# A graph-attention and expert kernel on one core: gathers without the other block's rows, one word of block numbers for two groups, and the message's wait last

## The chip, the cores and the metric

The kernel runs on one core of one Trainium2 chip. The core has five engines: PE (TensorE, matmuls), DVE (VectorE), ACT (ScalarE), POOL (GpSimd) and SP (SyncE, which only issues DMAs here), and 16 DMA engines. Each engine has a sequencer of its own that also carries out register operations, waits and branches. The metric is the device time of one execution in microseconds, the median of several runs: 3036.38 us before the change.

## The reference, cut to what matters

```python
def _gat_layer(x, W, attn_l, attn_r, bias, src, dst, num_heads, head_dim, use_elu):
    z = (x @ W).reshape(N, num_heads, head_dim)
    el = jnp.sum(z * attn_l, axis=-1); er = jnp.sum(z * attn_r, axis=-1)
    e = jax.nn.leaky_relu(el[src] + er[dst], 0.2)
    ex = jnp.exp(e - segment_max(e, dst)[dst])
    alpha = ex / segment_sum(ex, dst)[dst]
    out = segment_sum(alpha[:, :, None] * z[src], dst) + z + bias
    ...                                   # elu in the first two layers
x = x + gat(gat(gat(layernorm(x))))       # 3125 nodes, 768 wide, 50000 edges; heads 12, 12, 1
x = x + experts(layernorm(x))             # 8 experts, the best 2 of each token, 768 -> 192 -> 768
```

The edges are sorted by dst. Everything is float32.

## The kernel before

Each of the three graph layers is a *node sweep* and an *edge sweep*. The node sweep multiplies the 25 blocks of 128 nodes by W and stores z with its el (and a second, scaled el) as a row of a table in HBM. The edge sweep sums the messages. The rest (router, experts) comes after the third layer and isn't touched.

**Tiles and visits.** The 50000 sorted edges are 391 tiles of 128 edges. A tile whose edges end in two different blocks of destination nodes is *visited* twice, once for each block: 391 + 24 = 415 visits, `V`. Five visits are a group (`G`), 83 groups (`NG`) a layer; four groups are one turn of a hardware loop and have 20 buffers of rows (`U`). Block numbers of the visits aren't known when the program is built: they lie in `b_of` and are loaded into registers.

**One visit k**, in the order in which its data flow:
- POOL (line 672) gathers the 128 table rows of the tile's source nodes by an indirect DMA into buffer k mod 20, as soon as PE has added up visit k - 20 (semaphore `s_agg`). At a tile's second visit the same 128 rows are fetched again.
- PE (line 1022) fetches er of the edges' destinations by three small matmuls for each visit, with the transposed one-hot tile ST_b; it does so three groups ahead (`ER_LEAD`), for visits 0 and 1 behind visit 1 and for visits 2 to 4 behind visit 3, and then signals `s_er`.
- DVE (lines 1475 and 1480 in the layers with 12 heads, 1457 to 1469 in the last) makes the logits of a whole group; it waits for `s_er` and for the five gathers (`s_z`). ACT exponentiates (lines 821, 822).
- DVE (line 1492) multiplies each row by its weights, 768 numbers: the message, `s_msg`. In the last layer the weight goes into the one-hot tile instead (1494, 1498).
- For five or six visits of 20 (`SPLIT`) ACT and DVE split the row into a leading and a remaining part (781, 1509), so that PE adds it by four fast matmuls rather than by two slow ones; the semaphore is `s_rest`. These are called split visits here. SPLIT is places 2, 7, 10, 12, 17 of 20 in the first two layers and 1, 4, 7, 11, 14, 17 in the last.
- PE (line 1047) adds the row, turned by the one-hot tile S, onto the block's sums in PSUM, two halves of 384 or so. An edge of the other block has no 1 in its row of S, so its message is multiplied by zero.
- ACT (`close`) moves a finished block's sums out.

PE's program for a group is written out by `body`: load the block numbers of group g (`now`), visit 0, load those of group g + 3 (`later`), visit 1, six er matmuls, visits 2 and 3, nine er matmuls, visit 4. Ahead of each visit's matmuls stand its waits: the message or the rest, then `s_acc_free` (the block's sums are free, line 1042), and for visit 0 `s_S` (line 1044).

The tables by visit (`src_k`, `dst_k`, `b_of`) are made once, by DVE, ahead of the first node sweep; PE waits for them (`s_tables`).

Of the kernel before, what the change touches and what calls it, by code (L numbers as in the profile page):

```python
# [8 lines left out]
I32 = mybir.dt.int32  # L9
U32 = mybir.dt.uint32  # L10
U8 = mybir.dt.uint8
ALU = mybir.AluOpType
# [3 lines left out]
P = 128  # L16
N, D = 3125, 768
NE = 50000
NB = -(-N // P)
NPAD = NB * P  # L20
# [5 lines left out]
G = 5  # L26
NBUF = 4
IN_ARENA = 3
ER_LEAD = 3
U = G * NBUF  # L30
VISITS = ET + NB - 1
V = -(-VISITS // G) * G
NG = V // G
# [23 lines left out]
class Chain:  # L57
# [5 lines left out]
    def link(self, instruction):  # L63

        self.mark(instruction)
        self.follow()
# [33 lines left out]
def gnn_ffn(nc, x, edges, gnn, ffn, out):  # L100
    with ExitStack() as ctx:
        def sb(name, shape, dt=F32):
            return ctx.enter_context(nc.sbuf_tensor(name, shape, dt))
# [62 lines left out]
        src_k = sb("src_k", [P, V], I32)  # L166
        dst_k = sb("dst_k", [P, V])
        b_k = sb("b_k", [1, V + 1], I32)
        b_g = sb("b_g", [1, NG, 4], I32)
        b_of = sb("b_of", [1, NG + ER_LEAD, 8], I32)  # L170
        ends = sb("ends", [1, NB], I32)
        turns = sb("turns", [1, NS], I32)
# [171 lines left out]
        def prep(at, n):  # L344
            return ST[:, :, :, :].rearrange("p a b c -> p (a b c)")[:, at:at + n]
# [4 lines left out]
        def bk_f():  # L350
            return prep(V, V)
# [230 lines left out]
        def _(pool):  # L582
# [70 lines left out]
            for l in range(3):  # L653
                if l == 1:
                    pool.wait_ge(s_base, 16 * NB)
                    pool.wait_ge(s_spare, 16)
                    pool.wait_ge(s_last_bias, 16)
                if l == 2:
                    pool.wait_ge(s_bias_added, 16 * NB)
                sweep_nodes(pool, [(store(l), 0)])  # L660
                pool.wait_ge(s_stored[0], 16 * (NB // 2 + 1) * (l + 1))
                pool.wait_ge(s_stored[1], 16 * (NB // 2) * (l + 1))
                pool.wait_ge(s_tab, NB * (l + 1))
                pool.wait_ge(s_tables, 1)
                pool.wait_ge(s_filled, 16 * 2 * 3)
                pool.sem_inc(s_tick)
                for k in range(V):
                    pool.wait_ge(s_agg, V * l + k + 1)
                    if l == 2 and k == 12 * D // slot_width(l):
                        for q in range(2):  # L670
                            pool.wait_ge(s_x_kept[q], 16 * (NB // 2 + 1 - q))
                    nc.gpsimd.indirect_dma_start(  # L672
                        edge_row(l, k % U)[:, 0:table_width(l)], None, table[l][:, :],
                        bass.IndirectOffsetOnAxis(src_k[:, k:k + 1].bitcast(U32), 0)).then_inc(s_z[k % U], 16)

            for b in range(NB):
                keep_rows(b)
# [251 lines left out]
        def _(pe):  # L929
# [74 lines left out]
            def edge_sweep(l):  # L1004
# [5 lines left out]
                def blocks_of(g):  # L1010

                    return nc.values_load_multi_w_load_instructions(
                        b_of[0:1, bass.ds(g, 1), 0:G].rearrange("o i j -> o (i j)"), engines=[mybir.EngineType.PE],
                        min_val=0, max_val=NB - 1,
                        skip_runtime_bounds_check_because="b(k) is a sum of NB - 1 comparisons")[1]

                def er_of_edges(g, jj, j, b):

# [9 lines left out]
                def add_up(g, i, jj, j, b):  # L1028

                    at = jj * G + j  # L1030
                    odd = (b + l) % 2
                    flat = PS[:, :, :].rearrange("p b n -> p (b n)")
                    if at in SPLIT[l]:
                        n = SPLIT[l].index(at)
                        pe.wait_ge(s_rest, len(SPLIT[l]) * i + (n + 1 + split_before(l)))
                        onehot = S[:, jj, j, :]
                        rows = [parts[:, n, part, :] for part in range(2)]
                    else:
                        pe.wait_ge(s_msg, g * G + (V * l + j + 1))
                        onehot = f32(S[:, jj, j, :]) if H > 1 else S_weighted[:, jj, j, :]  # L1040
                        rows = [edge_row(l, at)]
                    pe.wait_ge(s_acc_free, b + (NB * l + 1))
                    if H > 1 and j == 0:
                        pe.wait_ge(s_S, g + (NG * l + 1))
                    for c, n in ((0, HALF), (1, sum_width(l) - HALF)):
                        for row in rows:
                            o = nc.tensor.matmul(flat[:, bass.ds(odd * 1024 + 512 * c, n)], onehot,  # L1047
                                                 row[:, c * HALF:c * HALF + n], start=False, stop=True, skip_group_check=True)
                    o.then_inc(s_agg, 1)

                def body(i, last):
                    groups = LAST_GROUPS if last else NBUF
                    for jj in range(groups):
                        g = NBUF * i + jj
                        ahead = not last or jj + ER_LEAD < groups
                        now = blocks_of(g)
                        for j in range(G):
                            add_up(g, i, jj, j, now[j])
                            if j == 0 and ahead:
                                later = blocks_of(g + ER_LEAD)  # L1060
                            if j in (1, 3) and ahead:
                                for n in ((0, 1), (2, 3, 4))[j // 2]:
                                    er_of_edges(g + ER_LEAD, (jj + ER_LEAD) % NBUF, n, later[n])

                pe.wait_ge(s_erm, l + 1)
                for g in range(ER_LEAD):
                    now = blocks_of(g)
                    for j in range(G):
                        er_of_edges(g, g, j, now[j])
# [129 lines left out]
        def _(dve):  # L1199
# [61 lines left out]
            link(nc.vector.tensor_copy(b_of[0:1, 0:NG, 0:G], starts))  # L1261
# [16 lines left out]

            def tables():
                dve.wait_ge(s_turned, 1)  # L1280
                link(nc.vector.tensor_copy(src_k[:, :], PS[:, 2, 0:V]))
                link(nc.vector.scalar_tensor_tensor(out=dst_k[:, :], in0=bk_f(), scalar=-float(P), in1=PS[:, 3, 0:V],
                                                    op0=ALU.mult, op1=ALU.add))
                if V > VISITS:
                    link(nc.vector.memset(dst_k[:, VISITS:V], NO_NODE))
                dve.sem_inc(s_tables, 1)

            W_parts = [(l, k, j) for l in (1, 2) for k in range(KC) for j in range(2)]
# [150 lines left out]
            def edge_sweep(l):  # L1439
# [8 lines left out]
                def exponents(g, i, jj):  # L1448
# [28 lines left out]

                    def higher():
                        dc.follow()
                        nc.vector.tensor_tensor(t, u, wu[:, :, H:2 * H], ALU.max).then_inc(s_pre, 1)  # L1480

                    if H > 1:
                        return both_logits, higher
# [376 lines left out]
```

## Time and profile before

| | us |
|---|---|
| median of 3 runs | 3036.38 |
| lowest, highest | 3032.83, 3039.52 |
| span of the profiled execution (no other time of it is given) | 3059.8 |
| PE busy in it | 2691.3 (88%) |
| DVE, POOL, ACT busy | 2096.8 (69%), 1506.0 (49%), 1244.9 (41%) |
| mean granted clock of PE, as a share | 0.964 |
| HBM read and written | 640.01 MB and 133.45 MB |

The span lies 0.8% over the median. It is counted from the first instruction to the last of one execution taken by the hardware profiler. Ends of matmuls are modelled, since they are pipelined, so a busy PE need not be one at its peak; the same matmul appears as several records. "Issue" is time in which an engine waited for nothing that the profile shows: its sequencer was at something else. "Remote" or "unknown queue" is a release whose event isn't among the recorded ones.

### The profile page before, as it was taken

Reading aid. Unit: us, or ns where it says so; the run is one execution under the profiler, and the core shown is the slowest. Engines: PE = TensorE matmul, PEld = TensorE weight load, DVE = VectorE, ACT = ScalarE, POOL = GpSimd, SP = SyncE. Lnnn points to the kernel's source line nnn. Section 1 sums busy time; section 2 is a strip of 40 time slices with the busy share of each in tenths; the row PEclk is TensorE's granted clock in tenths of the full one; section 3 lists DMA queues with packets and bytes.
Section 4 is the critical chain, followed back from the end, with each engine's and each line's share of the span. In section 5 each row is a group of like instructions: output and inputs, shape, how many; then the busy total and the mean of one; then the engine's idle time right before and its main releaser. Section 6 shows DMA issues by size and latency. Waiting matters only on the chain.

```text
span 3059.8 us, 57119 instructions
## 1 busy us (share of the span) xinstructions
PE 2691.3 (88%) x14056; PEld 1838.6 (60%) x14060; DVE 2096.8 (69%) x3895; ACT 1244.9 (41%) x2607; POOL 1506.0 (49%) x1528
## 2 busy tenths in 40 slices
PE   3997999998989979898989999788898889759998
PEld 2884555555558855555555578555555555547776
DVE  6776888888887768888878877545555555673332
ACT  1224555555544435555555544223222223622211
POOL 1005666666631156666666412466666665114443
PEclk9998999999999979999999999899999999979999
DMA  6447888888867878888888767788888887967776
GB/s 210 169 148 251 289 286 291 291 290 290 289 219 205 210 228 292 289 287 290 291 287 288 250 191 216 218 281 285 279 282 281 282 282 258 397 217 145 145 146 118
DMA packets 199261, 762.09 MB, mean 249 GB/s; under 512 B 41889, under 2 KB 58033, under 8 KB 198542
## 3 DMA queue, kind: packets, MB, share of 16 engines
q0 software_dynamic: 127632, 604.14, 64.8%
q1 hardware_dynamic: 53790, 108.21, 11.6%
q10 hardware_dynamic: 17760, 48.79, 4.0%
q8 instruction: 36, 0.59, 0.1%
q14 instruction: 43, 0.35, 0.0%
HBM read 640.01 MB, written 133.45 MB: 253 GB/s over the span
## 4 chain that ended last, share of the span: by engine, by line
PE 50%; DVE 21%; issue 13%; ACT 4%; DMA 4%; another core or an unknown queue 3%; SPq 2%; POOL 1%; DVEq 1%; ACTq 1%; POOLq 0%
PE PS L1047 30%; DVE arena L1492 5%; PE PS L1176 5%; PE PS L978 4%; PE PS L1165 4%; PE PS L980 2%; DVE parts L1509 2%; PE PS L1022 2%; DMA arena<-table,src_k 2%; SPq L493 1%; DVE ST_b L1445 1%; DVE arena L1357 1%; DVE arena L1367 1%; DVE arena L1335 1%
## 5 line engine op out<-in xcount | busy, mean ns | idle before, releaser
L672 POOL DMA_INDIRECT arena<-table,src_k x945 | 959.9, 1016 | 500.8 <-issue 213.1
L1047 PE MATMUL PS<-arena,S 128*128 128x384 f32 (+1 forms) x1848 | 706.8, 514 | 57.8 <-issue 46.3
L1492 DVE TENSOR_TENSOR arena<-arena,PS 128x768 f32<-128x768 f32 x630 | 575.2, 946 | 0.9 <-ACT arena L822 0.9
L1047 PEld LDWEIGHTS PS<-arena,S 128*128 128x128 f32 x1848 | 335.5, 194 | 282.7 <-issue 156.8
L1047 PE MATMUL PS<-parts,S 128*128 128x384 f32 (+2 forms) x1332 | 340.4, 375 | 57.2 <-issue 51.0
L672 POOL DMA_INDIRECT W<-table,src_k x300 | 295.9, 986 | 160.5 <-PE PS L1047 71.2
L1047 PE MATMUL PS<-arena,S_weighted 128*128 128x384 f32 (+1 forms) x840 | 319.9, 516 | 33.4 <-issue 25.3
L1022 PEld LDWEIGHTS PS<-erp,ST_b 128*128 128x128 bf16 x3735 | 193.9, 97 | 249.9 <-issue 184.2
L618 POOL DMA_DIRECT2D table<-arena x75 | 41.6, 555 | 557.7 <-DVEq L1379 382.3
L1047 PEld LDWEIGHTS PS<-parts,S 128*128 128x128 f32 x1332 | 223.7, 192 | 106.0 <-issue 97.5
L830 ACT ACTIVATE apart<-iota_row,dst_k 128x128 f32<-128x128 f32 x830 | 261.7, 389 | 60.8 <-issue 44.1
L781 ACT ACTIVATE parts<-arena 128x780 fp32r<-128x780 f32 x168 | 142.0, 849 | 309.2 <-DVE arena L1492 136.7
L1022 PE MATMUL PS<-erp,ST_b 128*128 x3735 | 213.0, 172 | 54.0 <-issue 38.9
L1047 PE MATMUL PS<-W,S 128*128 128x396 f32 (+1 forms) x640 | 239.8, 502 | 14.6 <-issue 8.1
L1047 PEld LDWEIGHTS PS<-arena,S_weighted 128*128 128x128 f32 x840 | 154.3, 196 | 143.7 <-issue 79.4
L978 PE MATMUL PS<-W_lead,S 128*128 128x512 f32 x450 | 190.4, 423 | 9.8 <-DVE xT_rest L1383 7.9
L1509 DVE TENSOR_TENSOR parts<-arena,parts 128x780 fp32r<-128x780 f32 x168 | 162.0, 964 | 35.7 <-issue 24.4
L1492 DVE TENSOR_TENSOR W<-W,PS 128x768 f32<-128x768 f32 x200 | 182.4, 944 | 0.0
L978 PE MATMUL PS<-W_lead,xT_rest 128*128 128x512 f32 x450 | 179.2, 398 | 0.0
L978 PE MATMUL PS<-W_rest_r,S 128*128 128x512 f32 x450 | 178.7, 397 | 0.0
L1047 PEld LDWEIGHTS PS<-W,S 128*128 128x128 f32 x640 | 116.1, 190 | 91.3 <-issue 39.0
L1795 DVE TENSOR_SCALAR arena<-PS,gate_of 128x768 f32<-128x768 f32 x56 | 57.0, 1018 | 162.5 <-PE PS L1176 162.5
(293 smaller groups left out, 4354.1 us busy)
## 6 DMA issues: line engine op xcount, KB each, us to landing
arena<-mixed SPq DMA_DIRECT2D x63, 384.0 KB, 3.6
table<-arena POOLq DMA_DIRECT2D x50, 396.0 KB, 3.3
local_b<-local SPq DMA_DIRECT2D x123, 160.0 KB
mixed<-sums ACTq DMA_DIRECT2D x50, 384.0 KB
arena<-table SPq DMA_DIRECT2D x50, 384.0 KB, 4.6
arena<-table,src_k POOLq DMA_INDIRECT x945
table<-arena POOLq DMA_DIRECT2D x25, 384.5 KB, 4.6
out<-last_bias POOLq DMA_DIRECT2D x25, 384.0 KB, 6.4
```

The costliest lines, as they stand in the source:

```text
L672: nc.gpsimd.indirect_dma_start(edge_row(l, k % U)[:, 0:table_width(l)], None, table[l][:, :], bass.IndirectOffsetOnAxis(src_k[:, k:k + 1]. ...
L781: nc.scalar.activation(parts[:, n, 0, 0:D + H], row[:, 0:D + H], ACT.Copy).then_inc(s_leading, 1)
L830: o = nc.scalar.activation(apart[:, j, :], iota_row[:, :], ACT.Abs, scale=-1.0, bias=dst_k[:, bass.ds(g * G + j, 1)])
L978: nc.tensor.matmul(PS[:, 4 + 2 * b.q, :], rows[x_part], W_parts[W_part][:, 0:512], start=start, stop=stop)
L980: o = nc.tensor.matmul(PS[:, 5 + 2 * b.q, 0:z_width(l) - 512], rows[x_part], W_parts[W_part][:, 512:z_width(l)], start=start, stop=stop)
L1022: o = nc.tensor.matmul(er_of(l, jj)[:, j, :], ST_b[:, jj, j * P:(j + 1) * P], erp[:, bass.ds(b * (6 * H) + part * 2 * H, 2 * H)], start=(p ...
L1047: o = nc.tensor.matmul(flat[:, bass.ds(odd * 1024 + 512 * c, n)], onehot, row[:, c * HALF:c * HALF + n], start=False, stop=True, skip_grou ...
L1165: o = nc.tensor.matmul(to, token_xT(b.q)[:, k * P:(k + 1) * P], WiT[:, k, bass.ds(e * FF, FF)], start=(k == 0), stop=(k == KC - 1))
L1176: o = nc.tensor.matmul(PS[:, 4 + 2 * b.q + c, 0:HALF], hT(b.q)[0:rows, j * P:(j + 1) * P], flat[0:rows, bass.ds(e * (2 * D) + (2 * c + j) ...
L1492: nc.vector.tensor_tensor(z, z, a, ALU.mult).then_inc(s_msg, 1)
L1509: nc.vector.tensor_tensor(low[:, 0:D + H], row[:, 0:D + H], f32(high[:, 0:D + H]), ALU.subtract).then_inc(s_rest, 1)
L1795: nc.vector.tensor_scalar(zr(b.q, D).rearrange("p (c d) -> p c d", c=2), PS[:, 4 + 2 * b.q:6 + 2 * b.q, 0:HALF], gate_of[:, bass.ds(b.n, 1 ...
```

## The change

1. `src_k`: from visit 20 on, an edge that isn't of the visit's block gets 3200 added to its source number, and the gather gets a bound (`bounds_check`), beyond which a row isn't fetched. What was in the buffer stays there; the one-hot tile multiplies it by zero as before.
2. `b_of` holds for each visit the block number and, times 256, that of the visit three groups on. PE loads five words at the head of a group and takes the one by a mask and the other by a shift; the load behind visit 0 goes.
3. In `add_up` the waits for `s_acc_free` and `s_S` stand ahead of those for the message or the rest.
4. The higher of the two logits is also limited to 0, in the same instruction, so that what is left in a buffer can't overflow. b_g and turns become bytes.

```diff
-        b_of = sb("b_of", [1, NG + ER_LEAD, 8], I32)
+        b_of = sb("b_of", [1, NG, 8], I32)
...
-                        bass.IndirectOffsetOnAxis(src_k[:, k:k + 1].bitcast(U32), 0)).then_inc(s_z[k % U], 16)
+                        bass.IndirectOffsetOnAxis(src_k[:, k:k + 1].bitcast(U32), 0),
+                        bounds_check=NPAD - 1, oob_is_err=False).then_inc(s_z[k % U], 16)
...
+                def now(word):
+                    return (word & (LOW - 1)).with_bounds(min_val=0, max_val=NB - 1)
+
+                def later(word):
+                    return (word >> 8).with_bounds(min_val=0, max_val=NB - 1)
...
+                    pe.wait_ge(s_acc_free, b + (NB * l + 1))
+                    if H > 1 and j == 0:
+                        pe.wait_ge(s_S, g + (NG * l + 1))
                     if at in SPLIT[l]:
...
-                    pe.wait_ge(s_acc_free, b + (NB * l + 1))
-                    if H > 1 and j == 0:
-                        pe.wait_ge(s_S, g + (NG * l + 1))
...
-                        now = blocks_of(g)
+                        words = blocks_of(g)
                         for j in range(G):
-                            add_up(g, i, jj, j, now[j])
-                            if j == 0 and ahead:
-                                later = blocks_of(g + ER_LEAD)
+                            add_up(g, i, jj, j, now(words[j]))
                             if j in (1, 3) and ahead:
                                 for n in ((0, 1), (2, 3, 4))[j // 2]:
-                                    er_of_edges(g + ER_LEAD, (jj + ER_LEAD) % NBUF, n, later[n])
+                                    er_of_edges(g + ER_LEAD, (jj + ER_LEAD) % NBUF, n, later(words[n]))
...
+            link(nc.vector.scalar_tensor_tensor(out=b_of[0:1, 0:NG - ER_LEAD, 0:G], in0=blocks[:, ER_LEAD:, :], scalar=float(LOW),
+                                                in1=blocks[:, 0:NG - ER_LEAD, :], op0=ALU.mult, op1=ALU.add))
...
-                link(nc.vector.tensor_copy(src_k[:, :], PS[:, 2, 0:V]))
...
+                link(nc.vector.tensor_copy(src_k[:, 0:U], PS[:, 2, 0:U]))
+                below, beyond = prep(2 * V, V - U), prep(3 * V, V - U)
+                link(nc.vector.tensor_scalar(below, dst_k[:, U:], 0.0, float(NPAD), ALU.is_lt, ALU.mult))
+                link(nc.vector.tensor_scalar(beyond, dst_k[:, U:], float(P), float(NPAD), ALU.is_ge, ALU.mult))
+                link(nc.vector.tensor_tensor(below, below, beyond, ALU.add))
+                link(nc.vector.tensor_tensor(src_k[:, U:], below, PS[:, 2, U:V], ALU.add))
...
-                        nc.vector.tensor_tensor(t, u, wu[:, :, H:2 * H], ALU.max).then_inc(s_pre, 1)
+                        nc.vector.scalar_tensor_tensor(out=t, in0=u, scalar=0.0, in1=wu[:, :, H:2 * H],
+                                                       op0=ALU.min, op1=ALU.max).then_inc(s_pre, 1)
```

PE's program at the head of the loop over groups, layer 0, visits 0 and 1 of its first group, before (ISA and REGISTER_ALU are register operations; a wait stands with the instruction that carries it):

```order
L1012 TENSOR_LOAD b_of
L1039 ISA
L1042 REGISTER_ALU [waits s_msg]
L1044 REGISTER_ALU [waits s_acc_free]
L1047 ISA [waits s_S]
L1047 MATMUL PS<-arena,S 128x384
L1047 ISA
L1047 MATMUL PS<-arena,S 128x396
L1012 ISA
L1012 TENSOR_LOAD b_of
L1039 REGISTER_ALU
L1042 REGISTER_ALU [waits s_msg]
```

The same place now:

```order
L1014 TENSOR_LOAD b_of
L1041 REGISTER_ALU x2
L1043 REGISTER_ALU [waits s_acc_free]
L1050 ISA [waits s_S]
L1055 ISA [waits s_msg]
L1055 MATMUL PS<-arena,S 128x384
L1055 ISA
L1055 MATMUL PS<-arena,S 128x396
L1041 REGISTER_ALU x2
L1050 REGISTER_ALU [waits s_acc_free]
L1055 ISA [waits s_msg]
```

The second load and the operation ahead of it are gone, the mask is the first of the two REGISTER_ALU of line 1041, and the message's wait has moved behind the others, to the operation just ahead of the matmul.

DVE's making of the tables, ahead of the first node sweep, before:

```order
L1342 TENSOR_TENSOR W_rest_r<-W,W_lead 128x792 [waits s_W_lead] x5
L1281 CAST src_k<-PS 128x415 [waits s_turned]
L1282 SCALAR_TENSOR_TENSOR dst_k<-ST,PS 128x415 [waits s_dve]
L1402 MEMSET gm 128x12 [waits s_dve]
L1310 BN_STATS stats<-arena 128x6 [waits s_in0,s_dve]
```

And now:

```order
L1290 SCALAR_TENSOR_TENSOR dst_k<-ST,PS 128x415 [waits s_turned]
L1294 CAST src_k<-PS 128x20 [waits s_dve]
L1296 TENSOR_SCALAR ST<-dst_k 128x395 [waits s_dve]
L1297 TENSOR_SCALAR ST<-dst_k 128x395 [waits s_dve]
L1298 TENSOR_TENSOR ST<-ST 128x395 [waits s_dve]
L1299 TENSOR_TENSOR src_k<-ST,PS 128x395 [waits s_dve]
```

One pass over the source numbers became five instructions, four of them over 395 columns, each waiting for the one before.

## Rows read from the trace of the kernel before

**Rows 1.** Windows: stretch, length, busy us by engine (instructions), clock, DMA share, GB/s

```profile
256.00:857.00 601.00, 541.90 (x2681) 323.56 (x2682) 497.63 (x717) 326.42 (x780) 397.83 (x392) 0.97 0.88 289
1100.00:1730.00 630.00, 555.03 (x2803) 333.80 (x2804) 523.23 (x757) 339.59 (x806) 415.30 (x411) 0.97 0.88 287
1945.00:2610.00 665.00, 582.00 (x2934) 357.50 (x2933) 351.06 (x1106) 186.87 (x409) 415.07 (x418) 0.96 0.86 277
...
2601.00:2677.50 76.50, 56.04 (x377) 39.40 (x377) 51.53 (x136) 46.20 (x83) 10.91 (x20) 0.91 1.01 397
```

**Rows 2.** Chain of waits, shares by line: first, second and third edge sweep

```profile
by line: PE PS L1047 59.5%; issue 13.2%; DVE arena L1492 7.6%; another core or an unknown queue 4.1%; PE PS L1022 4.1%; DVE parts L1509 3.0%; DMA arena<-table,src_k 2.4%; DVE W L1492 1.8%; DVE ST_b L1445 1.7%; POOL arena L672 0.8%; DVE wt L
by line: PE PS L1047 28.9%; issue 18.3%; DVE arena L1492 16.3%; another core or an unknown queue 6.4%; DVE parts L1509 6.2%; DVE W L1492 4.4%; DMA arena<-table,src_k 4.0%; POOL arena L672 3.6%; DVE ST_b L1445 3.5%; PE PS L1022 1.7%; DVE wt 
by line: PE PS L1047 50.1%; issue 24.5%; another core or an unknown queue 3.7%; PE PS L1022 3.6%; DMA arena<-table,src_k 3.0%; ACT parts L785 2.1%; DVE S_weighted L1498 1.4%; DVE ST_b L1445 1.3%; ACTq L790 1.0%; DVE parts L1513 0.9%; POOL a
```

**Rows 3.** Waits of PE from 306 to 765 us: total us, times, longest

```profile
PE PS L1047 <- issue: 31.4, 75, 3.7
PE PS L1022 <- issue: 6.6, 15, 0.9
PE PS L1047 <- DVE arena L1492: 0.7, 3, 0.3
```

**Rows 4.** PE's register operations by line: ns min/median/max, first and last start

```profile
L1012 PEldq TENSOR_LOAD <-b_of x498: 5/582/1751, 249.9 to 2596.9; - x166
L1042 PEldq ALU_OP  x1245: 2/32/737, 260.9 to 2601.5; - x178
```

**Rows 5.** PE in order of time, layer 0, then layer 2: start, us, work

```profile
470.01 0.97 PE L1047 MATMUL PS<-parts,S 128*128 128x384 f32 x4
471.25 1.57 PE L1047 MATMUL PS<-arena,S 128*128 128x384 f32 x4 [0.27 <-issue]
...
472.81 0.95 PE L1047 MATMUL PS<-parts,S 128*128 128x384 f32 x4
473.60 1.47 PE L1047 MATMUL PS<-arena,S 128*128 128x384 f32 x4
...
2100.22 1.16 PE L1047 MATMUL PS<-parts,S 128*128 128x384 f32 x4
2101.23 0.45 PE L1022 MATMUL PS<-erp,ST_b 128*128 x6
```

**Rows 6.** PE's weight loads in order of time, with the idle time before

```profile
704.33 0.62 PEld L1047 LDWEIGHTS PS<-arena,S 128*128 128x128 f32 x3 [0.33 <-issue]
```

**Rows 7.** DMA queues: packets, MB, share of the 16 engines' span

```profile
q0 software_dynamic: 127632, 604.14, 64.8%
```

**Rows 8.** DVE's waits before its logits: us, times

```profile
  remote: 142.3, 85
  DMA arena<-table,src_k: 26.2, 17
```

**Rows 9.** POOL's indirect DMAs: by line, and in order of time

```profile
L672 POOL DMA_INDIRECT arena<-table,src_k x945: 941/950/1745, 246.3 to 2588.6; - x189
...
L650 POOL DMA_INDIRECT out<-arena,target_of x56 | 89.1, 1591 | 159.2 <-DMA out<-arena,target_of 124.6 <-DVE arena L1795 30.1 <-issue 4.5
L635 POOL DMA_INDIRECT arena<-normed,token_of x56 | 55.0, 983 | 53.3 <-DVE token_of L1747 30.7 <-issue 16.5 <-PE PS L1149 6.2
...
510.38 0.95 POOL L672 DMA_INDIRECT arena<-table,src_k  x1 [0.30 <-issue]
```

**Rows 10.** DVE ahead of the first node sweep, in order of time

```profile
51.16 0.58 DVE L1281 CAST src_k<-PS 128x415 int32<-128x415 f32 x1
...
54.24 0.56 DVE L1310 BATCH_NORM_STATS2 stats<-arena 128x6 f32<-128x384 f32 x1 [1.63 <-DMA arena<-in_x]
```

**Rows 11.** DVE's two forms over five columns

```profile
L1461 DVE SCALAR_TENSOR_TENSOR wu<-wu 128x5 f32<-128x5 f32 x83 | 13.5, 162 | 0.0
...
L1457 DVE TENSOR_TENSOR wu<-arena,PS 128x5 f32<-128x5 f32 x63 | 10.3, 164 | 151.6 <-remote 123.2 <-issue 17.7 <-DMA arena<-table,src_k 10.6
```

More of the change, by code:

```diff
@@ L29 @@
 ER_LEAD = 3
+LOW = 256
 U = G * NBUF
@@ L168, in gnn_ffn @@
         b_k = sb("b_k", [1, V + 1], I32)
-        b_g = sb("b_g", [1, NG, 4], I32)
-        b_of = sb("b_of", [1, NG + ER_LEAD, 8], I32)
+        b_g = sb("b_g", [1, NG, 4], U8)
+        b_of = sb("b_of", [1, NG, 8], I32)
         ends = sb("ends", [1, NB], I32)
-        turns = sb("turns", [1, NS], I32)
+        turns = sb("turns", [1, NS], U8)
         erm = sb("erm", [P, NB, 2 * HMAX])
@@ L1013, in blocks_of @@
                         b_of[0:1, bass.ds(g, 1), 0:G].rearrange("o i j -> o (i j)"), engines=[mybir.EngineType.PE],
-                        min_val=0, max_val=NB - 1,
+                        min_val=0, max_val=(NB - 1) * (LOW + 1),
                         skip_runtime_bounds_check_because="b(k) is a sum of NB - 1 comparisons")[1]
+                def now(word):
+                    return (word & (LOW - 1)).with_bounds(min_val=0, max_val=NB - 1)
+                def later(word):
+                    return (word >> 8).with_bounds(min_val=0, max_val=NB - 1)
                 def er_of_edges(g, jj, j, b):
@@ L1055, in body @@
                         ahead = not last or jj + ER_LEAD < groups
-                        now = blocks_of(g)
+                        words = blocks_of(g)
                         for j in range(G):
-                            add_up(g, i, jj, j, now[j])
-                            if j == 0 and ahead:
-                                later = blocks_of(g + ER_LEAD)
+                            add_up(g, i, jj, j, now(words[j]))
                             if j in (1, 3) and ahead:
                                 for n in ((0, 1), (2, 3, 4))[j // 2]:
-                                    er_of_edges(g + ER_LEAD, (jj + ER_LEAD) % NBUF, n, later[n])
+                                    er_of_edges(g + ER_LEAD, (jj + ER_LEAD) % NBUF, n, later(words[n]))
                 pe.wait_ge(s_erm, l + 1)
                 for g in range(ER_LEAD):
-                    now = blocks_of(g)
+                    words = blocks_of(g)
                     for j in range(G):
-                        er_of_edges(g, g, j, now[j])
+                        er_of_edges(g, g, j, now(words[j]))
                 with pe.Fori(0, NI - 1) as i:
@@ L1260, in _ @@
             link(nc.vector.memset(b_of[0:1, :, :], 0))
-            link(nc.vector.tensor_copy(b_of[0:1, 0:NG, 0:G], starts))
+            link(nc.vector.tensor_copy(b_of[0:1, :, 0:G], starts))
+            blocks = bk_f()[0:1, :].rearrange("o (g j) -> o g j", j=G)
+            link(nc.vector.scalar_tensor_tensor(out=b_of[0:1, 0:NG - ER_LEAD, 0:G], in0=blocks[:, ER_LEAD:, :], scalar=float(LOW),
+                                                in1=blocks[:, 0:NG - ER_LEAD, :], op0=ALU.mult, op1=ALU.add))
             link(nc.vector.tensor_copy(ends[0:1, 0:NB - 1], enter[0:1, :]))
```

## The prediction

> **What bounds the kernel now.** I read the page's slices and the windows by stage first, then the chain of waits stage by stage, then PE's row of instructions inside a sweep, and last POOL and DVE. The windows show five stretches [rows 1]: the three edge sweeps take 601, 630 and 665 us, 1896 of 3059.8, and the other stages hardly touch what the change touches. In a sweep three things are close to full at once: PE is busy 88 to 90%, the 16 DMA engines 86 to 88%, DVE 83% in two sweeps and 53% in the third. So busy shares don't decide it; the chain does. In the three sweeps it runs through PE's adding matmuls, the er matmuls and "issue" for 77, 49 and 78% [rows 2], 68% on average, and through landings of gathers ("DMA arena<-table" and "unknown queue") for 6.5, 10.4 and 6.7%, which is 39 + 66 + 45 = 150 us. PE first, landings second.
>
> "Issue" on PE is worth a look: PE waits for no other engine there (31.4 us before its adding matmuls in one 459 us window, 0.7 us for DVE's messages [rows 3]). The register instructions of its sequencer stand between the matmuls: a load of block numbers lasts 582 ns (498 of them), an ALU operation 32 ns, both up to 0.7 us and more at times [rows 4].
>
> **The load that goes.** Before, each group of five visits has two loads, one ahead of visit 0 and one behind it; after, one, ahead of visit 0. 498 loads become 3 x (3 + 83) = 258, so 240 go, 240 x 0.582 = 140 us of the sequencer. Most of that is hidden, since a visit of plain matmuls gives the array 1.3 us of work. It shows where the load meets a split visit, which is short: the split visit at 472.81 is followed after 0.79 us, the one at 470.01, which has the later load behind it, after 1.24 us with 0.27 idle [rows 5]. That is 0.45 us. In layers 0 and 1 it holds for places 10 of 20, about 21 groups each; in layer 2 the split visit is the one behind the load (places 1 and 11), where the er matmuls that need the load start 2101.23 - 2100.22 = 1.01 us behind the split visit instead of 0.79, 0.22 us; about 42 groups. 42 x 0.45 + 42 x 0.22 = 28 us. Bounds: 0, if something else is late there anyway, and 140.
>
> The Trainium skill (page "Runtime: NRT & Kernel Launch", section Instruction fetch mechanics) puts a register load at about 200 ns for each register, even in bulk; for five words that would be 1.0 us a load and 240 us for the 240. The row has 0.58 us for five words, so the measurement decides and I leave the page's figure out of the sum.
>
> **The register operations that come.** Each visit gets one more (the mask), in the order's listing five a group; the shift for the er matmuls takes a place that was there. Lower bound: 0, hidden under the array. Upper: idle of the weight loads before a visit, 0.33 us where nothing else is late [rows 6], holds three such operations, so about 0.1 us each; it can only show behind the nine er matmuls, once a group, 249 x 0.1 = 25 us. I take the instruction's own 32 ns: 8 us.
>
> **Pauses.** Operations of 32 ns that last 0.7 us [rows 4] are stalls of the sequencer that no engine explains. A sequencer with 0.58 - 5 x 0.1 = 0.1 to 0.58 - 5 x 0.03 = 0.4 us a group to spare recovers from some. PE's idle before lines 1047 and 1022 is 31.4 + 6.6 us in that window [rows 3], 38 of 459, so about 157 in 1896. I give 13 of them back. Bounds 0 and 80.
>
> These three, -28 + 8 - 13 = -33, count where PE is on the chain, 68%: **-22 us**. Behind a faster PE the next that is late is DVE, at 497.63 of 601 us in the first sweep [rows 1].
>
> **The waits reordered.** s_acc_free and s_S now stand ahead of s_msg. They are met long before in nearly every visit; behind the message's wait there are then one operation less or two, 0.1 us, and PE waits for a message 3 times in the window, 0.7 us [rows 3]. Queued behind the wait are this visit's matmuls and the next er matmuls, as before. -1 us, bounds 0 and -10.
>
> **Gathers with rows left out.** There are 415 visits for 391 tiles, so 24 tiles are visited twice; the first 20 visits stay whole, which leaves 23 pairs. A pair now fetches each row once: 23 x 128 + 48 rows of padding = 2992 rows a layer of 53120, 5.6%; at 3168 and 3076 bytes 28.2 MB of the queue's 604.14. That queue's packets took 64.8% of the engines' span, 1983 us, or 3.28 us for a MB [rows 7], so 93 us of transfers go. What of it lies on the chain? Landings are 150 us of it; 5.6% of that is **-8 us**. DVE's waits before its logits are booked mostly to "remote", 142.3 us, and only 26.2 us to a gather [rows 8], so a late gather isn't proven as their cause; the s_er semaphore is in the same wait. Bounds 0 and -93.
>
> By the Trainium skill ("DMA: Bandwidth & Descriptors", section Anatomy of one DMA) a DMA from POOL costs about 2.0 us fixed and bytes / 436 GB/s. The fixed part stays for a gather of half the rows; the 28.2 MB would be worth at most 65 us, not 93. The case with full gain below would shrink by that much.
>
> POOL's instruction itself: 950 ns at the median, and 0.30 us of issue between two [rows 9]. PE's pace is 1896 / 1245 = 1.52 us a visit, so POOL has 0.27 us to spare a visit. That a check of 128 indices costs POOL something is not in the trace. Bounds: 0 (the same instruction with one more field; below nothing too, if fewer rows mean fewer descriptors, with no effect, as POOL waits anyway), and the scatter's 1591 ns. I take 0, since the other indirect read, of another width, stands at 983 ns.
>
> **Ahead of the first sweep.** b_of gets one more pass over 400 numbers (0.58 us, as the row of 415 columns in [rows 10]); the table of sources becomes five instructions instead of one: 0.58 goes, four of nearly 0.58 and a short one come, some +2.0 us [rows 10]. PE waits for s_tables, but DVE's next work, on the first rows of x, starts at 54.24 after a wait of 1.63 us for them, which takes up most of it. So +1.0 us; bounds 0 and 2.6. DVE's min-and-max in place of max: a two-operation form of 5 columns has 162 ns against 164 [rows 11], so 0.
>
> **Sum.** -22 - 1 - 8 + 1 = -30 us against the profiled 3059.8, which becomes 3030. The profiled execution lies 23 us over the median of 3036.4; that part is the same in both, so 3036.4 - 30 = **3006 us**, 1.0% less.
>
> **Rivals.** (A) The forecast, 50%, with a range of its own from 2980 to 3029.
> (B) Landings and DMA traffic bound the sweeps: 88% busy engines and the "remote" waits speak for it, a stretch with 1.01 and 397 GB/s elsewhere [rows 1] against it. Then the 93 us come in full, and half of A's PE part: 3036 - 93 - 11 = 2932. 12%.
> (C) Nothing to measure: the sequencer's saved loads are spent on 1245 more operations, each 0.1 us (125 us against 140), and the rows left out shorten gathers that were in time: -5 to +5, 3036. 20%.
> (D) Slower, on POOL: with the bounds check the gather's instruction passes 1.22 us; from there POOL is the pace of a sweep. At the scatter's 1.59 + 0.30 = 1.89 us the sweeps take 1245 x 1.89 = 2353 us, +457; at 1.35 + 0.30, 1245 x 0.13 = +162. Against it: the program has the same number of POOL instructions, and an index compare is small. 7%, at about 3200.
> (E) Slower, on PE's sequencer: the operations land where they show, behind the nine er matmuls (+25), and the load's 0.45 us was not on the chain (0): 3036 + 25 - 9 = 3052. 11%.
> That rows are not left out at all (no index beyond the bound) is a case of C in time; the trace would show it in bytes.
>
> **How the numbers follow.** Measurement of this kernel tells 0.2%, 6 us, from nothing. Faster: A, B and a little of C, 66%. Same: most of C, 16%. Slower: D, E, 18%. The range for 8 in 10 reaches down towards B and up over C and E: 2935 to 3050.
>
> **What would show it.** Right: 258 loads of b_of; the split visit with the later load followed after 0.8 us, not 1.24; PE's "issue" in the sweeps down by some tens of us; software queue at about 576 MB; L673's instruction still at 950 ns with longer waits for PE. Wrong: a gather instruction over 1.2 us (D); bytes unchanged; the visit behind nine er matmuls 0.1 us later than before and PE's issue no smaller (C, E); sweeps shorter by 30 us each with DVE's "remote" wait gone (B). If PE's rows improve and the sweeps don't shorten, what I took for PE's chain was a loop through DVE and POOL.

## The result: 2.0% slower, and the profile after

The changed kernel takes 3097.5 us against 3037.1 of the kernel before, ratio 1.0201 (95% interval 1.0185 to 1.0216). The forecast was 3006, so it was wrong in sign: 60 us lost instead of 30 gained.

The windows of the three edge sweeps after (stretch, length, busy us by engine, clock, DMA share, GB/s), against [rows 1]:

```profile
256.00:868.00 612.00, 546.08 (x2707) 332.20 (x2707) 494.09 (x723) 328.57 (x781) 431.14 (x394) 0.95 0.84 272
1112.00:1750.00 638.00, 559.30 (x2776) 338.99 (x2776) 512.49 (x748) 337.35 (x799) 440.56 (x406) 0.95 0.83 267
1970.00:2645.00 675.00, 579.54 (x2928) 359.50 (x2926) 349.62 (x1106) 185.25 (x408) 449.84 (x417) 0.94 0.81 258
```

Of the 40 us between the two profiled executions 29 lie in these: the sweeps are 11, 8 and 10 us longer, DMA is 4 to 5 points less busy, and POOL 33, 25 and 35 us busier. No other engine comes near that: PE's matmuls are 4, 4 and -2 us busier, at a clock that fell by 0.02. The page's rows of the software queue and of the gathers (count, busy us, mean ns, idle before), against [rows 7]:

```profile
q0 software_dynamic: 127632, 576.01, 62.2%
...
L673 POOL DMA_INDIRECT arena<-table,src_k x945 | 1024.1, 1084 | 453.6 <-issue 244.2
...
L673 POOL DMA_INDIRECT W<-table,src_k x300 | 330.5, 1102 | 142.5 <-issue 73.7
```

and by duration (min/median/max ns), against [rows 9]:

```profile
L673 POOL DMA_INDIRECT arena<-table,src_k x945: 992/1002/1791, 247.6 to 2623.7; - x189
```

The rows that the change leaves out are left out: 576.0 MB, as forecast. But each gather's instruction takes 1.00 us at the median instead of 0.95, and on the mean of all 1245 it takes (1024.1 + 330.5) / 1245 = 1.088 us. The same two rows of the page before read:

```profile
L672 POOL DMA_INDIRECT arena<-table,src_k x945 | 959.9, 1016 | 500.8 <-issue 213.1
...
L672 POOL DMA_INDIRECT W<-table,src_k x300 | 295.9, 986 | 160.5 <-PE PS L1047 71.2
```

That is (959.9 + 295.9) / 1245 = 1.009 us, so the mean went up by 79 ns, 99 us of POOL in all. The median went up by 52 ns; the other 27 ns of the 79 are long gathers. POOL and DVE after, in order of time, at one of them:

```profile
338.11 1.01 POOL L673 DMA_INDIRECT W<-table,src_k  x1 [0.30 <-issue]
339.42 1.70 POOL L673 DMA_INDIRECT arena<-table,src_k  x1 [0.30 <-issue]
341.42 1.13 POOL L673 DMA_INDIRECT arena<-table,src_k  x1 [0.30 <-issue]
```

```profile
339.26 0.96 DVE L1524 TENSOR_TENSOR parts<-arena,parts 128x780 fp32r<-128x780 f32 x1
```

The gather of 1.70 us lies beside DVE's rest. Of the 1245 gathers 34 took over 1.5 us before and 89 after, and every one of them, in both traces, overlaps a rest (lines 1509, 1513 before; 1524, 1528 after).

Who waits for it: DVE before the logits of the first two layers, after (us, times), against [rows 8]:

```profile
  remote: 115.3, 42
  DMA arena<-table,src_k: 61.1, 36
  DMA W<-table,src_k: 30.4, 18
```

and in the third layer, after and then before:

```profile
  remote: 90.5, 26
  DMA arena<-table,src_k: 64.0, 23
...
  DMA W<-table,src_k: 17.5, 9
```

```profile
  remote: 150.5, 57
...
  DMA arena<-table,src_k: 10.6, 4
  DMA W<-table,src_k: 2.1, 1
```

Waits for gathers went from 26.2 for those into arena [rows 8], 7.2 for those into W and 12.7 in the third layer, 46 us, to 173 us; "remote" fell from 293 to 206. The net of the two is 40 us of DVE idle, and the profiled span grew by 3099.3 - 3059.8 = 39.5. (The profiled span before lay 23 us over the median, that of after 2 us, so the profiles show 40 of the 60 us.)

Why 0.05 us matter though POOL had 0.27 us to spare: POOL's row after 500 us shows how it works.

```profile
507.26 1.00 POOL L673 DMA_INDIRECT arena<-table,src_k  x1 [1.54 <-remote]
508.57 1.00 POOL L673 DMA_INDIRECT arena<-table,src_k  x1 [0.31 <-issue]
509.88 1.01 POOL L673 DMA_INDIRECT arena<-table,src_k  x1 [0.30 <-issue]
511.19 1.01 POOL L673 DMA_INDIRECT arena<-table,src_k  x1 [0.30 <-issue]
512.50 1.01 POOL L673 DMA_INDIRECT arena<-table,src_k  x1 [0.30 <-issue]
513.81 1.00 POOL L673 DMA_INDIRECT arena<-table,src_k  x1 [0.30 <-issue]
515.12 1.01 POOL L673 DMA_INDIRECT arena<-table,src_k  x1 [0.30 <-issue]
518.16 1.00 POOL L673 DMA_INDIRECT arena<-table,src_k  x1 [2.03 <-remote]
```

It waits for PE in lumps, then issues a run of gathers 1.31 us apart (1.26 before, [rows 9]). Within the sweeps POOL's pauses of over 0.6 us went from 271, 356 us in sum, to 160, 255 us: about what its instructions gained. The time to spare sits in these pauses, ahead of a run and not inside it; as I read it, a run that takes longer delays the gather that the next logits wait for.

PE after: 258 loads of b_of instead of 498 [rows 4]:

```profile
L1014 PEldq TENSOR_LOAD <-b_of x258: 3/583/1450, 251.2 to 2633.4; - x129
```

and a split visit of place 10 followed sooner than in [rows 5], after 535.84 - 534.83 = 1.01 us instead of 1.24 (these are also the medians of the 42 such places in the first two layers; 0.8 was forecast):

```profile
534.83 1.17 PE L1055 MATMUL PS<-parts,S 128*128 128x384 f32 x4
535.84 1.47 PE L1055 MATMUL PS<-arena,S 128*128 128x384 f32 x4
```

Yet PE's "issue" did not fall by tens of us, it rose. Ahead of the adding and the er matmuls, over the whole run, before:

```profile
  issue: 136.5, 283
...
  issue: 38.9, 70
```

and after:

```profile
  issue: 159.0, 197
...
  issue: 52.1, 98
```

That is 175 us before and 211 after. PE's waits for DVE ahead of the same matmuls went from 41 to 32 us. So PE idles more, but not in a wait for DVE that the profile shows; the last link of the chain, from DVE's late logits to PE, is not seen in it.

### The profile page after: what moved, and what is told of

It reads as the page before. It is cut to its first block, busy times and chain, and to the rows that moved or that the text cites. A ratio compares the mean times of both kernels' runs of the same rounds, so it can differ in the third digit from the quotient of the medians.

```text
span 3099.3 us, 59281 instructions
## 1 busy us (share of the span) xinstructions
PE 2707.5 (87%) x14059; PEld 1859.8 (60%) x14060; DVE 2083.7 (67%) x3900; ACT 1246.7 (40%) x2607; POOL 1604.9 (52%) x1528
## 3 DMA queue, kind: packets, MB, share of 16 engines
q0 software_dynamic: 127632, 576.01, 62.2%
## 4 chain that ended last, share of the span: by engine, by line
PE 60%; issue 13%; DVE 12%; DMA 5%; POOL 4%; ACT 2%; another core or an unknown queue 1%; ACTq 1%; DVEq 0%; POOLq 0%; SPq 0%
PE PS L1055 35%; PE PS L980 7%; PE PS L1182 5%; PE PS L982 4%; PE PS L1171 4%; POOL arena L673 3%; PE PS L1030 3%; DVE arena L1507 3%; DMA arena<-table,src_k 3%; PE PS L1155 1%; PE PS L965 1%; DVE parts L1524 1%; DVE arena L1381 1%; DVE arena L1349 1%
## 5 line engine op out<-in xcount | busy, mean ns | idle before, releaser
L673 POOL DMA_INDIRECT arena<-table,src_k x945 | 1024.1, 1084 | 453.6 <-issue 244.2
L1055 PE MATMUL PS<-arena,S 128*128 128x384 f32 (+1 forms) x1848 | 715.8, 522 | 57.6 <-issue 43.7
L1055 PEld LDWEIGHTS PS<-arena,S 128*128 128x128 f32 x1848 | 348.3, 198 | 273.3 <-issue 133.4
L673 POOL DMA_INDIRECT W<-table,src_k x300 | 330.5, 1102 | 142.5 <-issue 73.7
L832 ACT ACTIVATE apart<-iota_row,dst_k 128x128 f32<-128x128 f32 x830 | 263.2, 389 | 39.9 <-issue 26.2
L651 POOL DMA_INDIRECT out<-arena,target_of x56 | 89.0, 1590 | 159.2 <-DMA out<-arena,target_of 128.1
```

What stands on the lines that cost most here:

```text
L651: nc.gpsimd.indirect_dma_start(out[:, :], bass.IndirectOffsetOnAxis(target_of[:, n:n + 1].bitcast(U32), 0), zr(n % 2, D), None, compute_op ...
L673: nc.gpsimd.indirect_dma_start(edge_row(l, k % U)[:, 0:table_width(l)], None, table[l][:, :], bass.IndirectOffsetOnAxis(src_k[:, k:k + 1]. ...
L832: o = nc.scalar.activation(apart[:, j, :], iota_row[:, :], ACT.Abs, scale=-1.0, bias=dst_k[:, bass.ds(g * G + j, 1)])
```

## The experiments

The runs fell on two kinds of chip, and this has to be told to read them. On some chips the kernel before takes 3034 to 3037 us, as in the result; on others, with the same program, 2805 to 2812. Each run has the kernel before beside it, so ratios are within one kind. I call them the first and the second kind (chips 3 and 12; chips 0, 2 and 9). An expectation that gives no time for the second kind was written for the first. Kernels built from the kernel before needed its tables of block numbers as bytes, so the first run prices that. "The PE part" is the changed kernel without the bound and without the rows left out.

| run | kind | us | before | ratio (95%) |
|---|---|---|---|---|
| e0 byte tables | 1 | 3065.5 | 3034.3 | 1.0105 (1.0090-1.0121) |
| e1 e0 + bound | 1 | 3114.6 | 3034.3 | 1.0262 (1.0248-1.0276) |
| e3 e1 + rows left out | 1 | 3116.6 | 3034.3 | 1.0276 (1.0257-1.0294) |
| e2 PE part | 1 | 3042.5 | 3034.3 | 1.0027 (1.0015-1.0039) |
| e12 e2, old order | 1 | 3044.8 | 3036.7 | 1.0027 (1.0015-1.0038) |
| e13 e2, two loads | 1 | 3082.0 | 3036.7 | 1.0154 (1.0140-1.0168) |
| e9 e2 + memset 1 | 1 | 3050.3 | 3035.2 | 1.0046 (1.0032-1.0060) |
| e11 e2 + memset 64 | 1 | 3065.5 | 3036.7 | 1.0097 (1.0082-1.0112) |
| e10 changed kernel | 1 | 3100.6 | 3035.2 | 1.0218 (1.0201-1.0235) |
| e14 half of the rows | 1 | 3098.9 | 3036.7 | 1.0209 (1.0195-1.0223) |
| e5 e2, old order | 2 | 2808.3 | 2808.5 | 1.0003 (0.9989-1.0018) |
| e6 e2, two loads | 2 | 2941.8 | 2808.5 | 1.0481 (1.0462-1.0499) |
| e7 e2 + a met wait | 2 | 2808.2 | 2808.5 | 1.0002 (0.9987-1.0016) |
| e8 half of the rows | 2 | 2902.2 | 2808.5 | 1.0335 (1.0316-1.0354) |
| e15, e17 e2 + 2nd mask | 2 | 2818.5, 2822.2 | 2804.7, 2811.5 | 1.0058, 1.0047 (each +-0.002) |
| e16, e18 e2 + memset 96 | 2 | 2933.0, 2939.4 | 2804.7, 2811.5 | 1.0465, 1.0455 (each +-0.002) |

**Which part loses (e0 to e3).** The edits are `b_g`, `turns`, `b_of` to U8 (e0); with it

```diff
+                        bounds_check=NPAD - 1, oob_is_err=False).then_inc(s_z[k % U], 16)
```

(e1); with it the five instructions for `src_k` and the limited logit (e3); and the changed kernel with all of these taken out again (e2).

> The kernel before with b_g, turns and b_of as bytes instead of 32-bit numbers, and nothing else; the next kernels that leave PE's program as it was are built on it. All theories: no difference, 3030 to 3044 us (ratio 0.998 to 1.002), POOL's gather at 0.95 us. If it is slower, the byte tables have a part in the 60 us.

> Byte tables, and the bound on the gathers alone; no row lies beyond it, so every gather still moves 128 rows, and PE's program is that of before. Theory POOL (the bound makes each gather's instruction 0.05 us longer, 1.00 instead of 0.95; five of them follow each other once PE has signalled, so the logits come 0.25 us later a group, and PE's pauses that come of it let its clock fall): nearly all of the loss, 3080 to 3110 us, clock 0.95. Theory PE (the loss is in PE's masks and in the waits' new order): 3037 us, clock 0.964, though the gather stands at 1.00. Theory rows (buffers that are half filled, packets without data): 3037 us.

> The changed kernel without the bound and without the rows left out: one load of packed words a group, masks and shifts, the message's wait last, byte tables. Theory POOL: no loss, and what the load gives back, 3005 to 3040 us, clock 0.96. Theory PE: 3085 to 3100 us, clock 0.95. Theory rows: as theory POOL.

> Byte tables, the bound and the rows left out (576 MB in the software queue), with the higher logit limited to 0; PE's program is that of before. Theory POOL: as the bound alone, at most 10 us less, 3070 to 3105 us. Theory PE: 3020 to 3037 us. Theory rows: 3090 to 3105 us while the bound alone stays at 3037.

The bound alone costs 1.0262 - 1.0105 = 1.6%, 48 us, and on the other base, with the rows left out, 1.0201 or 1.0218 less 1.0027, 53 to 58 us. The rows left out give nothing (3114.6 and 3116.6). Both lie over the ranges expected for them (3110 and 3105 at most), since these counted nothing for the byte tables. The PE part loses 8 us instead of gaining, 3042.5 where theory POOL had 3040 at most. e10 repeats the changed kernel and came out as expected (3097). e0 was expected at no difference and cost 31 us: a load of five bytes takes twice as long as one of five words.

```profile
L1012 PEldq TENSOR_LOAD <-b_of x498: 431/1222/2616, 251.8 to 2598.1; - x166
```

498 x (1.222 - 0.582) = 319 us of the sequencer cost 31 us. The gathers of e1, all of 128 rows, and no row beyond the bound:

```profile
L672 POOL DMA_INDIRECT arena<-table,src_k x945 | 1024.7, 1084 | 482.9 <-issue 255.9
...
L672 POOL DMA_INDIRECT W<-table,src_k x300 | 330.1, 1100 | 134.2 <-issue 77.0
```

the same as after. So the length comes with the bound, not with rows left out. I had also thought that PE's lower clock (0.964 to 0.950) was a step of the loss. The clock doesn't order the times (e2 3042 us at 0.960, e1 3115 us at 0.968), so it isn't the cause. It did fall with the bound on either base, from 0.975 in e0 to 0.968 in e1 and from 0.960 in e2 to 0.950, while PE's matmuls became 20 and 15 us busier; that a part of this size goes through the clock is not excluded.

**Is it POOL's time (e7, e9, e11, e16, e18)?** e7 puts a second, met wait ahead of each gather; the others

```diff
+                    nc.gpsimd.memset(spare_column[:, :], 0)
```

of 1, 64 or 96 columns, whose result nothing reads.

> The PE part, and on POOL ahead of each gather, behind PE's signal, a second wait on a semaphore that was met long ago, so about 0.05 us more from gather to gather without any bound. Theory POOL (what the bound costs is its 0.05 us on POOL, five in a row between PE's signal and the next group's logits): 3085 to 3100 us, clock 0.95. Rival (the bound costs in the DMA queue or in descriptors, not as time of POOL): 3042 to 3050 us.

> The PE part (no bound, no rows left out) with a memset of one column on POOL ahead of each gather, which does nothing for the result. The earlier delay by a second wait added nothing from gather to gather, so it told nothing. Theory POOL: the gathers follow each other later by what the memset takes (from 0.03 to 0.1 us each); on a chip where the kernel before takes 3034 us the loss is about 1 us for each ns, as with the bound (0.05 us for 50 us); where it takes 2808 us and POOL had no pause at all between gathers, 1245 times the added time, so 1.2 us for each ns. Rival (the bound costs in other ways than POOL's time): no loss on the first kind of chip.

> The PE part with a memset of 64 columns on POOL ahead of each gather. The memset of one column (0.12 us) fitted into the 0.30 us that POOL takes between two gathers anyway, so their starts stayed 1.26 us apart and the time rose by 8 us only; one of 64 columns should take 0.17 to 0.18 us and bring the starts to 1.30 to 1.33 us, as far apart as with the bound (1.31). Theory POOL: where the kernel before takes 3035 us, 3085 to 3105 us. Rival (the bound costs in other ways than POOL's time): 3050 to 3058 us. Where before takes 2808 us: 2860 to 2900 us by theory POOL.

> The PE part with the memset on POOL ahead of each gather widened from 64 to 96 columns, so that the starts of two gathers in a row should be 1.31 to 1.32 us apart, as with the bound (1.31), against 1.26 without and 1.29 with 64 columns (which cost 23 us over the PE part). Theory POOL, at 0.7 us for each ns and visit: 3075 to 3095 us. Rival (the bound costs in more ways than by the starts): 3065 to 3072 us. Where before takes 2808 us: 2870 us or so.

> The PE part with the memset of 96 columns ahead of each gather, again; its starts were 1.31 us apart in a row of gathers, as with the bound. Where before takes 3036 us: theory POOL 3075 to 3100 us, as the changed kernel; rival (the bound costs in more ways than by the starts) 3065 to 3072 us. Where before takes 2805 us: 2933 us again.

e7 added nothing, since the gathers stayed 1.25 us apart (0.95 + 0.30), and so says nothing. One column fits into the 0.30 us as well, and costs 6 us all the same. 64 columns bring the starts to 0.17 + 0.16 + 0.96 = 1.29 us:

```profile
507.51 0.96 POOL L677 DMA_INDIRECT arena<-table,src_k  x1
508.47 0.17 POOL L676 MEMSET spare_column<- 128x64 uint8 x1
508.79 0.96 POOL L677 DMA_INDIRECT arena<-table,src_k  x1 [0.16 <-issue]
```

No bound, the gather itself unchanged (959.2 + 299.4 over 1245 = 1.011), starts 26 ns further apart at the median (1.283 against 1.257 in e2), and 1.0097 - 1.0027 = 0.7%, 21 us, or 15 more than with one column: 0.6 to 0.8 us for each ns. The bound puts the starts 54 to 57 ns further apart and makes the mean gather 77 ns longer (1.088 against 1.011 in e2); by this rate that is 32 to 62 us, and 48 to 58 were measured. So time of POOL alone costs something, and of the right size. It doesn't show that the bound costs nothing else: e11's 3065.5 us lies between the range of theory POOL (3085 at least) and that of the rival (3058 at most), and misses both. The wider memset, which was to try it at 50 ns, fell twice on the second kind of chip.

There it cost 128 us (2870 in all was expected, 2933 came). POOL hardly waits for PE there: its pauses of over 0.6 us inside the sweeps are 2 in e5 and 16 in e16, against 271 in the kernel before on the first kind. The starts are 1.31 us apart and more beside a rest, and the mean of gather, memset and gap is 1.052 + 0.203 + 0.16 = 1.41 us against 1.024 + 0.30 in e5: 1245 x 0.09 = 112 of the 128 us. With what pauses there are, the mean from start to start is 1.43 against 1.33 us, which is all of it. So on that kind the pace of the sweeps is POOL's (e16, in order of time):

```profile
506.89 0.96 POOL L677 DMA_INDIRECT arena<-table,src_k  x1 [0.16 <-POOL spare_column L676]
507.84 0.20 POOL L676 MEMSET spare_column<- 128x96 uint8 x1
508.21 0.96 POOL L677 DMA_INDIRECT arena<-table,src_k  x1 [0.16 <-POOL spare_column L676]
```

**Are bytes worth anything (e8, e14)?** On the changed kernel, half of all rows left out; half of the sum over edges is missing from its output.

```diff
+                link(nc.vector.memset(src_k[0:64, U:V], NPAD))
```

> The changed kernel in which from visit 20 on the rows of partitions 0 to 63 lie beyond the bound as well, so that only half of the rows are fetched (about 330 MB in the software queue); leaves out half of the sum over edges. Theory POOL (the gather's instruction and its place set the pace, the bytes don't): 3085 to 3097 us, instruction still 1.00 us. Theory transfers (landings bound the sweeps): 240 MB less at 3.28 us is 790 us of transfers, and the time falls by 100 us or more, until PE alone bounds it.

> The changed kernel with the rows of partitions 0 to 63 left out as well, again; leaves out half of the sum over edges. Where before takes 3035 us: theory POOL 3085 to 3100 us; theory transfers, or any part of the landings on the chain, 3000 us or under. Where before takes 2808 us: 2902 us again.

On the first kind 3098.9 us, as the changed kernel, with 224 MB less:

```profile
q0 software_dynamic: 127632, 352.22, 40.4%
```

The packets are as many as before. On the second kind 94 us over the kernel before, no faster for its lost bytes; its gathers take 1.105 us on the mean against 1.024 in e5, and 1245 x 0.081 = 101 us. So the bound's longer instruction is the whole loss there, and on neither kind are the bytes on the path. When a gather lands still matters, as DVE's waits for it show.

**What became of PE's gain (e5, e6, e12, e13, e15, e17).** Old order of waits; the second load back behind visit 0, with both words masked; a second mask ahead of each visit:

```diff
-                    return (word & (LOW - 1)).with_bounds(min_val=0, max_val=NB - 1)
+                    return ((word & (LOW - 1)) & 127).with_bounds(min_val=0, max_val=NB - 1)
```

> The PE part (one load of packed words, masks and shifts, byte tables b_g and turns; no bound, no rows left out; 3042 us before) with the waits in their old order: the message first. Theory order (the new order costs, since the hardware puts the message's wait behind the register operations that were hidden by it): back to 3034 us or under. Theory masks (the added mask ahead of each visit costs what the load gives): 3042 us or over. If the new order helps as forecast: 3043 to 3052 us.

> The PE part with the second load of a group back behind visit 0 (32-bit words, all masked), waits in the new order: what removing 240 loads of 0.58 us is worth. By the forecast of 28 us x 0.68 = 19 us: 3061 us. By the rate of the byte tables (498 loads longer by 0.64 us each cost 31 us, 0.097 us for a us of load; 240 x 0.58 = 140 us of loads): 14 us, 3056 us. If the loads are hidden: 3042 us.

> The PE part with the waits in their old order, again, since in the first run the chip was one on which POOL bounds the sweeps and PE's part can't show. Where before takes 3035 us: 3034 us or under if the new order costs something, 3042 us if neither order matters, 3043 to 3052 us if the new order helps as forecast. Where before takes 2808 us: 2808 us again.

> The PE part with the second load back, all words masked, again. Where before takes 3035 us: 3061 us by the forecast of 19 us for the loads, 3056 us by the rate of the byte tables, 3042 us if the loads are hidden. Where before takes 2808 us: 2942 us again, so PE becomes the bound there with two loads and the mask.

> The PE part with a second mask behind the first one ahead of each visit, so one more register operation of 0.03 us in the place where the change added one; nothing else. Theory masks (what the load gives, the added mask takes back: two loads with both words masked stood 45 us over the kernel before, for 2490 masks, half of them ahead of visits): 3060 to 3090 us where before takes 3036 us. Rival (32 ns are hidden under the array, as forecast at 8 us): 3042 to 3050 us. Where before takes 2808 us: 2808 us, or more if masks make PE the bound there.

> The PE part with a second mask ahead of each visit, again, since the last run fell on a chip where POOL bounds the sweeps (2818 beside 2805 us there: the mask began to show even so). Where before takes 3036 us: theory masks 3060 to 3090 us; if 32 ns are hidden, 3042 to 3050 us. Where before takes 2805 us: 2818 us again.

The order of the waits is worth nothing on either kind (on the second, e7 has the new order). The second load, which brings 1245 masks of their own ahead of the er matmuls with it in place of the shifts, costs 39 us on the first kind, more than any of the three times expected, and 133 on the second, where POOL waits for PE again (186 pauses of over 0.6 us). But then two loads with masks stand 45 us over two loads without (e13 against before), and masks are what they differ in (beside the order, which is worth nothing, and byte tables on ACT, whose load takes 473 ns instead of 494). On the second kind a second mask costs 11 to 14 us though POOL sets the pace. On the first kind its price wasn't measured, since both runs fell on the other.

The traces hold the price that was overlooked. A mask is busy for 32 to 36 ns, but in every trace, of either kind, the next operation starts some 60 ns after the end of one where nothing is waited for, so from start to start it is 92 to 97 ns. The shift is no free one either: it goes into the operation ahead of the first er matmul of a visit, which takes 85 to 93 ns instead of 46 to 52. So the change takes 240 loads from PE's sequencer, with what stands ahead of them and the 60 ns some 176 us, and gives it 1245 x 0.097 = 121 us of masks and 1200 x 0.04 = 48 us of shifts. The two sides nearly cancel. What that is worth in time is an estimate: e13 has 2490 masks more than the kernel before, some 239 us of the sequencer, for 45 us, so the 169 us of masks and shifts are worth about 32 us; and of the 39 us between e13 and e2 the load alone has some 28. Where the later load stood, visit 11 starts 0.81 us after visit 10 in e2 (median of 42), as forecast, but 1.36 in e13 against 1.24 before.

## Why the prediction was wrong

**POOL's instruction, taken at 0** is the step that failed. The bound makes it 0.05 us longer at the median and 0.08 on the mean, and alone costs 48 to 58 of the 90 us between forecast and result. The nearest rows (983 ns for another gather) were read as if a check cost nothing; they show no bound at all. The second half of the mistake is the threshold in rival D: the loss was to begin when a gather passes 1.22 us, POOL's 1.52 us of pace less 0.30. It began at once, some 1 us for each ns (48 to 58 us for the median's 52), with a fifth of the way to the threshold used up. That it did so because POOL is not served at an even pace fits POOL's row and DVE's waits; on the first kind of chip the way from there to PE is argued. D had the right engine and the right instruction; only on the second kind was POOL the pace of the sweeps, as D says.

**Gathers with rows left out, -8 us**: 0. e1 and e3, and half of all rows in e14, show that bytes don't matter. The 3.28 us for a MB was no price of a MB either: 28.1 MB less took 1983 - 0.622 x 3099.3 = 55 us off the engines' packets, not 93.

**The load that goes, -28 x 0.68 = -19 us**: right in kind. With the masks of its own that the second load brings it is 39 us; for the load alone I estimate 28.

**The register operations that come, +8, and the pauses, -13**: the second step that failed. The PE part as a whole is +8 us where -19 + 5 - 9 - 1 was the forecast for it, so something took back some 32 us. The term took a mask at its own 32 ns and the shift at nothing; from start to start a mask is 97 ns and the shift adds 40, together 169 us of the sequencer and by the estimate above 32 us. The trace of the kernel before had this spacing. That they cost this much is worked out, not shown, as no run on the first kind has the change's load without its masks. The upper bound, +25, counted only one place a group. Rival C had the price right, 0.1 us for each of 1245 operations, and for the PE part it is C that came out. The sequencer's stalls, which the pauses were to give back, did not get fewer: operations of over 0.4 us (loads and branches left out) are 238 with 182 us before, 272 with 182 us in e2 and 400 with 270 us in the changed kernel. They grow with POOL's time without any bound too (316 in e9, 357 in e11). But between e0 and e1 they hardly do (67 and 70 us), and the bound costs 48 us there too, so the loss doesn't need them.

**The waits reordered, -1**: 0. **Ahead of the first sweep, +1**: first gathers at 246.3 and 247.6, so +1.3, right.

Of the signs that were to show it, PE's row did improve where the load went, PE's "issue" rose by 36 us instead of falling, and the sweeps did not shorten. The prediction reads this as a loop through DVE and POOL, where it had seen a chain through PE; DVE's waits for gathers, 46 to 173 us, fit that.

No version that I ran beats the kernel before on the first kind; on the second the PE part equals it (seen in e5 and e7).

## What to carry to other kernels

An engine with 15% to spare on average may have none where it counts: if its work comes in lumps (runs of gathers between waits), most of each ns that one takes more can be passed on (here 0.6 to 1.0 us in all for each ns of 1245 gathers). Before adding a field to an instruction that stands in such a row, find out its price; before saving bytes, halve them in a trial and see if the time moves. And one load less in a sequencer doesn't pay if an operation is added ahead of each of the matmuls it fed; price such an operation from its start to the start of the next, not by its own length.

## What the runs showed of the hardware

- The bound on an indirect DMA with 128 indices: instruction from 0.95 to 1.00 us, whether rows lie beyond it or not; left-out rows remain as packets (127632 with 604, 576 and 352 MB).
- A gather that runs beside DVE's 780-column rest takes up to 1.8 us, 0.8 more than the median. Beside a rest the mean is 1.08 us before and 1.19 after, elsewhere 0.97 and 1.03.
- Five bytes loaded into registers take 1.22 us, five words 0.58.
- After a register operation of 32 or 36 ns on PE's sequencer the next starts 60 ns later, on both kinds of chip, so it takes 92 to 97 ns of the sequencer.
- POOL's 0.30 us between two indirect DMAs takes in a met wait or a memset of one column: the starts stay 1.25 to 1.26 us apart.
- Chips differ by 8% on this kernel (3035 and 2808 us). Register operations of PE's sequencer, on the first kind (e2, the masks and what stands with them) and then the second (e5, where the same operations stand under another line):

```profile
L1040 PEldq ALU_OP  x2490: 2/36/1134, 260.7 to 2578.9; - x192
```

```profile
L1049 PEldq ALU_OP  x2490: 32/36/36, 262.6 to 2348.7; - x192
```

and PE's "issue" before its adding matmuls, in the same two runs:

```profile
PE PS L1054 <- issue: 131.2, 209, 5.6
```

```profile
PE PS L1054 <- issue: 11.6, 39, 0.9
```

On the first kind the sequencer stalls (272 operations of over 0.4 us in e2), on the second none of these operations does; what makes the stalls, and how much of the 8% is theirs, stays open.
